# Scores for the maxima half a step later in a cross-attention kernel: heads 0 and 1 at a step's end, heads 2 and 3 in the next step, and v's third part in two pieces

## The reference

```python
x = layer_norm(hidden_states, ln1_w, ln1_b)
q = heads(x @ q_w + q_b); k = heads(ctx @ k_w + k_b); v = heads(ctx @ v_w + v_b)
attn = softmax(where(mask, q @ k.T / sqrt(32), finfo.min))
hidden = heads_back(attn @ v) @ cproj_w + cproj_b + hidden_states
y = gelu(layer_norm(hidden, ln2_w, ln2_b) @ fc_w + fc_b) @ proj_w + proj_b   # 512 -> 2048 -> 512
return hidden + y
```

## Time and profile before

| | us |
|---|---|
| median of 3 runs (757.47 to 764.28) | 763.86 |
| the profiled execution | 761.63 |
| its span in the profile | 759.8 |

### The profile page before, as it was taken

The page is one execution under the profiler, slowest core; times in us unless marked ns, Lnnn a source line. Parts: engine busy times, 40 slices in busy tenths (PEclk is TensorE's granted clock), DMA queues, the critical chain, the costliest instruction groups (busy, mean ns, idle before and its releaser), DMA issues.

```text
span 759.8 us, 13142 instructions
## 1 busy us (share of the span) xinstructions
PE 701.7 (92%) x4544; PEld 607.5 (80%) x4544; DVE 465.2 (61%) x859; ACT 321.7 (42%) x582; POOL 257.5 (34%) x219
## 2 busy tenths in 40 slices
PE   3769989899998989899789999999999999999997
PEld 3658879798888879798677888888888888888886
DVE  5487978988789898978868775533225232252222
ACT  4146766867677776857751212112121121211110
POOL 6234656655546666556743121000000001000000
PEclk9787989999999999999889999999999999999999
DMA  7685554645455454434705400010001000010001
GB/s 222 158 239 149 161 159 123 166 141 156 139 155 153 140 155 138 113 114 142 196 1 161 130 1 1 15 41 1 1 0 56 0 0 0 0 55 1 1 0 57
DMA packets 51146, 69.16 MB, mean 91 GB/s; under 512 B 8344, under 2 KB 29208, under 8 KB 51104
## 3 DMA queue, kind: packets, MB, share of 16 engines
q1 hardware_dynamic: 50832, 68.07, 31.2%
q0 software_dynamic: 272, 0.54, 0.4%
HBM read 47.21 MB, written 20.99 MB: 90 GB/s over the span
## 4 chain that ended last, share of the span: by engine, by line
PE 70%; issue 9%; DVE 8%; POOL 6%; ACT 3%; DMA 3%; SPq 2%; DVEq 0%; ACTq 0%; POOLq 0%
PE psum L1212 8%; PE psum L1213 8%; PE psum L1214 8%; PE psum L1199 8%; PE psum L1198 8%; PE psum L1197 8%; PE psum L1004 6%; PE psum L1005 5%; PE psum L1006 5%; POOL p_lo L473 4%; PE psum L1038 2%; PE psum L1095 2%; DVE negm L755 2%; PE psum L1022 1%; PE psum L1116 1%
## 5 line engine op out<-in xcount | busy, mean ns | idle before, releaser
L473 POOL TENSOR_TENSOR p_lo<-p,p_hi 128x512 f16<-128x512 f32 x128 | 156.9, 1236 | 122.5 <-ACT p_hi L559 122.2
L685 ACT ACTIVATE h<-psum,cols 128x512 f32<-128x512 f32 x64 | 44.1, 689 | 290.0 <-PE psum L1199 290.0
L942 DVE CAST h_hi<-h 128x512 fp32r<-128x512 f32 x64 | 27.9, 436 | 208.1 <-ACT h L685 208.1
L557 ACT ACTIVATE p<-psum,maskbias 128x512 f32<-128x512 f32 x128 | 88.4, 690 | 45.8 <-PE psum L1022 44.8
L1212 PE MATMUL psum<-w_mlp,h_hi 128*128 128x512 f32 x256 | 100.7, 393 | 0.9 <-DVE hidden L784 0.9
L1214 PE MATMUL psum<-w_mlp,h_lo 128*128 128x512 f32 x256 | 99.7, 390 | 0.0
L1213 PE MATMUL psum<-w_mlp,h_hi 128*128 128x512 f32 x256 | 99.7, 389 | 0.0
L1197 PE MATMUL psum<-y_hi,w_mlp 128*128 128x512 f32 x256 | 99.7, 389 | 0.0
L1199 PE MATMUL psum<-y_hi,w_mlp 128*128 128x512 f32 x256 | 99.7, 389 | 0.0
L1198 PE MATMUL psum<-y_lo,w_mlp 128*128 128x512 f32 x256 | 99.6, 389 | 0.0
L559 ACT ACTIVATE p_hi<-psum,maskbias 128x512 f16<-128x512 f32 x128 | 88.8, 694 | 0.0
(11 more groups left out here) (105 smaller groups left out, 1516.1 us busy)
## 6 DMA issues: line engine op xcount, KB each, us to landing
qk_rows<-qk SPq DMA_DIRECT2D x32, 512.0 KB, 2.7
stacks<-qk_rows SPq DMA_DIRECT2D x64, 256.0 KB
stacks<-qk_rows SPq DMA_DIRECT2D x64, 128.0 KB
hidden<-in_x_dram SPq DMA_DIRECT2D x8, 512.0 KB, 4.5
ctx_sb<-in_ctx_dram SPq DMA_DIRECT2D x8, 512.0 KB, 5.2
w_mlp_raw<-in_L_xattn_fc_w_dram SPq DMA_DIRECT2D x16, 256.0 KB, 4.6
w_mlp_raw<-in_L_xattn_proj_w_dram SPq DMA_DIRECT2D x16, 256.0 KB, 6.2
out_dram<-hidden SPq DMA_DIRECT2D x16, 256.0 KB, 2.3
```

Source lines behind the costliest of these rows:

```text
L473: pool.tensor_tensor(p_lo[:, slot, :], p32[:, u % 2, :], p_hi[:, slot, :], ALU.subtract).then_inc(s["p_lo_done"], 1)
L557: act.activation(p32[:, u % 2, :], psum[:, ST + kc, :], ACT.Exp, bias=maskbias[:, kc:kc + 1], scale=SCALE32)
```

## The change

The scores of heads 0 and 1 move to the end of the step on PE, and those of heads 2 and 3 of the same group to the next step, just behind `transposed_scores` of the first pair. `transpose_max` moves from the front part of a step to its end: in steps 0 to 2 just ahead of the second pair of `transposed_scores`, in step 3 behind the scores. DVE's `maximum` calls move with them: heads 2 and 3, with the two `m12` operations, come right behind `low_parts`, and heads 0 and 1 are last in the step. ACT's copy to `mrow` moves behind the second pair of exponentials (in step 3, behind the third). The table `USES` gets a new order. The third part of v is made in two pieces, one in step 0, one at the start of step 1. The subtraction of v's rest (L909) moves ahead of `add_hidden` in step 3. No instruction of arithmetic is added or removed, and the orders of SP and POOL stay as they are.

```diff
-        USES = [("qk", 0), ("ctx", 0), ("ctx", 1), ("m", 0), ("c", 1),
-                ("qk", 1), ("m", 1), ("att", 0), ("att", 1), ("v", 0),
-                ("qk", 2), ("m", 2), ("v", 1),
-                ("qk", 3), ("m", 3), ("c", 0), ("x", 0), ("x", 1)]
+        USES = [("qk", 0), ("ctx", 0), ("ctx", 1), ("c", 1), ("m", 0),
+                ("qk", 1), ("att", 0), ("att", 1), ("v", 0), ("m", 1),
+                ("qk", 2), ("v", 1), ("m", 2),
+                ("qk", 3), ("c", 0), ("x", 0), ("m", 3), ("x", 1)]
```

In DVE's `step`:

```diff
             def step(it, g):
+                if g == 1 and batch(it):
+                    third_part(1)
                 low_parts(it, g)
...
                 if g == 0 and batch(it + 1):
                     context_lo(it, 0)
+                maximum(it, g, (2, 3))
+                if g == 0 and batch(it + 1):
                     context_lo(it, 1)
...
                 if g != 1:
                     products_out(it, g)
-                maximum(it, g, (0, 1))
...
                     wait(dve, "v_cast", it * 2 + 1)
-                    for kc in range(KC):
-                        ins = dve.tensor_tensor(vparts[:, kc, :, 1 + 2 * HD:VW], v_heads[:, kc],
-                                                vparts[:, kc, :, 1 + HD:1 + 2 * HD], ALU.subtract)
-                    ins.then_inc(s["v_split"], 1)
+                    third_part(0)
...
                     add_values(it, g - 1)
-                last = isinstance(it, int) and (it, g) == (B - 1, 0)
-                if last:
-                    maximum(it, g, (2, 3))
+                if g == 3 and batch(it + 1):
+                    wait(dve, "v1_cast", it + 2)
+                    dve.tensor_tensor(v32[:, :, :], v32[:, :, :], v1[:, :, :], ALU.subtract).then_inc(s["v_rest"], 1)
                 if g == 0 and batch(it - 2):
                     add_hidden(it, 1)
...
                 if g == 3 and batch(it + 2):
                     affine_x(it + 2)
-                if not last:
-                    maximum(it, g, (2, 3))
-                if g == 3 and batch(it + 1):
-                    wait(dve, "v1_cast", it + 2)
-                    dve.tensor_tensor(v32[:, :, :], v32[:, :, :], v1[:, :, :], ALU.subtract).then_inc(s["v_rest"], 1)
+                maximum(it, g, (0, 1))
```

In PE's `step`:

```diff
                 if g == 0:
                     transposes(it, "ctx", 0, it + 1, ctx_sb, "ctx_loaded", 16, "ctx_tr")
+                    scores(it, g, (2, 3))
                     values(it, g)
                     transposes(it, "ctx", 1, it + 1, ctx_sb, "ctx_loaded", 16, "ctx_tr")
-                    scores(it, g, (0, 1))
+                    project_c(it, 1)
                     transpose_max(it, g)
-                    if last:
-                        transposed_scores(it, g, 1)
-                        scores(it, g, (2, 3))
-                    project_c(it, 1)
...
+                scores(it, g, (0, 1))
                 if g == 3:
+                    transpose_max(it, g)
                     transposes(it, "x", 1, it + 2, xn, "x_normed", 2, "x_tr")
-                if not (last and g == 0):
-                    scores(it, g, (2, 3))
```

More of the change, by code:

```diff
@@ L640, in step @@
                     exps(it, g, 1)
-                    maxima_out(it, g)
-                    if batch(it + 1) and not (isinstance(it, int) and it == -1):
+                    if batch(it + 1):
                         x_hi(it + 1)
@@ L651, in step @@
                     exps(it, g, 1)
-                if g == 2:
+                if g >= 2:
                     exps(it, g, 0)
                     exps(it, g, 1)
[L655 to L658, removed]
+                if g != 3:
                     maxima_out(it, g)
@@ L662, in step @@
                 exps(it, g, 2)
+                if g == 3:
+                    maxima_out(it, g)
                 exps(it, g, 3)
@@ L696, in tail @@
                 if it == B and g == 1:
-                    wait(act, "v_split", B)
+                    wait(act, "v_split", B * 2)
                     gelu(0, 0)
@@ L746, in maximum @@
             def maximum(it, g, heads):
-                G = it * NG + g + 2
+                G = it * NG + g + (2 if heads[0] == 0 else 1)
                 if not group(G):
@@ L788, in add_values @@
                 wait(dve, "v_proj", b * 2 + (t + 1))
-                wait(dve, "v_split", b)
+                wait(dve, "v_split", b * 2)
                 dve.tensor_tensor(v32[:, t, :], in_bank("v", t), vb_bc[:, :], ALU.add).then_inc(s["v_added"], 1)
@@ L850, in products_out, with third_part @@
                     dve.reciprocal(rl[:, t, h0:h0 + GH], rows[:, :, 0]).then_inc(s["pv_taken"], 1)
+            def third_part(kc):
+                dve.tensor_tensor(vparts[:, kc, :, 1 + 2 * HD:VW], v_heads[:, kc],
+                                  vparts[:, kc, :, 1 + HD:1 + 2 * HD], ALU.subtract).then_inc(s["v_split"], 1)
             def step(it, g):
+                if g == 1 and batch(it):
+                    third_part(1)
                 low_parts(it, g)
@@ L868, in step @@
                     products_out(it, g)
-                maximum(it, g, (0, 1))
-                if g == 0 and batch(it + 1) and not (isinstance(it, int) and it == -1):
+                if g == 0 and batch(it + 1):
                     x_lo(it + 1)
@@ L1034, in scores @@
                 for hh in heads:
-                    h = GH * ((g + 2) % NG) + hh
+                    h = GH * ((g + (2 if heads[0] == 0 else 1)) % NG) + hh
                     wait(pe, "max_taken", G * 4 + (hh - 1))
@@ L1105, in values @@
                 wait(pe, "p_lo_done", (G + 1) * 4)
-                wait(pe, "v_split", b + 1)
+                wait(pe, "v_split", (b + 1) * 2)
                 wait(pe, "v_cast", (b + 1) * 2)
@@ L1142, in step @@
                     transposes(it, "ctx", 0, it + 1, ctx_sb, "ctx_loaded", 16, "ctx_tr")
+                    scores(it, g, (2, 3))
                     values(it, g)
                     transposes(it, "ctx", 1, it + 1, ctx_sb, "ctx_loaded", 16, "ctx_tr")
-                    scores(it, g, (0, 1))
+                    project_c(it, 1)
                     transpose_max(it, g)
-                    if last:
-                        transposed_scores(it, g, 1)
-                        scores(it, g, (2, 3))
-                    project_c(it, 1)
                 if g == 1:
-                    transpose_max(it, g)
-                    scores(it, g, (0, 1))
+                    scores(it, g, (2, 3))
                     for j in range(2):
@@ L1160, in step @@
                 if g == 2:
+                    scores(it, g, (2, 3))
+                    values(it, g)
+                    project_v(it, 1)
                     transpose_max(it, g)
+                if g == 3:
+                    scores(it, g, (2, 3))
                     values(it, g)
[L1163 to L1172, removed]
                     if last:
@@ L1178, in step @@
                     transposes(it, "x", 0, it + 2, xn, "x_normed", 2, "x_tr")
-                if not (last and g in (0, 3)):
+                if not (last and g == 3):
                     transposed_scores(it, g, 1)
```

## The result

The changed kernel takes 801.88 us (median of 4 runs, 798.04 to 806.07) against 760.87 us for the kernel before beside it: a ratio of 1.053, 95% interval 1.048 to 1.058. Its profiled execution took 798.07 us, with a span of 796.3 us against 759.8.

What follows compares the result with a forecast made beforehand. TensorE, busy 92%, loses wherever it newly waits for in-order DVE; step terms over the iterations sum to +30.4, plus 3 for the tail, on 761.6: 795, forecast 796 us with half the median's offset, range 774 to 818.

Steps and rivals of the forecast that it cites:

- Step 0: First step of a batch: project_qk newly waits for DVE's add_hidden, 12.9 against 11.11 us, +1.8 (+0.4 to +2.9).
- Step 1: PE's 1.7 us wait goes, but the v projection waits for low_parts: 11.3 against 11.90 us, -0.6 (-1.0 to 0).
- Step 2: project_qk newly waits for DVE's add_values: 11.0 against 9.02 us, +2.0 (+1.0 to +2.6).
- Step 3: transpose_max waits for add_hidden, project_qk for ACT's mrow copy: 12.6 against 10.72 us, +1.9 (+1.2 to +3.1).
- The batch: Four steps of a full batch in the loop, 42.75 us before: +1.8 - 0.6 + 2.0 + 1.9 = +5.1 us.
- the tail: Iteration 7: transposed_scores waits for the mrow DMA, some 2.8 us beyond cover in two or three steps; +3 (0 to +6).
- rival 2: The clock joins in: one lower-clock stretch in each of six batches, +10 us, up to 825 with high ends; chance 0.14.
- rival 1: POOL and DVE fall apart in time, so the terms are their low ends: +12 us, no tail, 774; chance 0.14.
- Rival 3: Faster, 749 us: DVE reaches v_added (9.0 us into step 2) and add_hidden (about 10 into step 0) before PE asks; chance 0.06.
- rival 4: No change, 762 us: new waits as long as the old ones, those in steps 2 and 3 hidden; chance 0.06.
- the signs named: PE waits at project_qk in steps 0, 2, 3, some 6 us per batch; step 1's transpose_max wait gone; DVE about 37 us.
- The rule weighed: DVE and POOL exclude each other for whole instructions: m12 pairs could be held twice, 4 to 5 us more per batch.

Runs made afterwards that it cites:

- a_all: Changed kernel with three DVE orders edited: add_values ahead of the statistics in step 2, add_hidden earlier in steps 0 and 3; 767.6 us, ratio 1.007.
- b_split: Kernel before with only v's third part in two pieces, the second at the start of step 1; 753.72 us, ratio 0.986.
- b_split_more: b_split repeated with more rounds, against the kernel before; 754.79 us, ratio 0.989.
- a_mrow: a_all plus ACT's copy to mrow ahead of the third pair of exponentials in step 3; 764.34 us, ratio 1.002.
- a_best: a_all plus ACT's mrow copy ahead of the third exponentials in step 3 and add_hidden ahead of x_lo in step 0; 767.55 us, ratio 1.003.
- a_step0: Changed kernel with add_hidden of step 0 ahead of the first piece of v's third part on DVE; 794.45 us, ratio 1.040.
- a_step3: Changed kernel with add_hidden of step 3 ahead of products_out and v's rest on DVE; 794.16 us, ratio 1.039.
- b_vrest: Kernel before with only the subtraction of v's rest moved ahead of add_hidden in step 3; 763.58 us, ratio 1.001.

## Why the prediction was right, point by point

*The bound.* DVE's order for the most part, and not its amount of work: three DVE edits took back 31 of 36.5 us of span, some 23 of them in the lengths of the steps. Theory B, that PE's placement or the `mrow` path costs the time, fails as the main cause in a_all, but something is left of it. The change contains b_split, which helps by itself. Beside that part alone (b_split_more, 754.79 us) the best form of the whole change (a_mrow, 764.34) is 9.6 us longer at nearly the same mean clock (0.971 and 0.974). By the windows its batch takes 43.46 us against 41.83, with steps 1 to 3 longer by 0.5, 0.8 and 0.5. Whether PE's placement, the new turns of the banks or more DVE orders make these 1.6 us wasn't tested.

*The terms, against the full-clock batch.* Step 0: +1.8 forecast, +1.33 found; `m12` was disturbed little there (0.39 for the cast) and `x_lo` took 1.27 instead of 1.6. Step 1: -0.6, found -0.38. Step 2: +2.0, found +2.46: the two `m12` operations took 0.72 and 1.08, near my high end, beside POOL. Step 3: +1.9, found +1.68; `normed_x` needed only 0.99 instead of 1.94 for both tiles, as POOL's pair ended when it began (286.52 and 286.46), but the `m12` subtraction ahead of it was held until then (1.09 instead of 0.17), which I had not counted in this step. The batch: 47.85 forecast, 47.84 found; the errors of the terms cancel, so the last digits are luck.

*The sum.* The start of iteration 0 came 2.1 us later (I had 0.5), iteration 0 was 1.1 us longer (3.2 forecast), iteration 1 by 4.9, iterations 2 to 5 by 7.5, 6.4, 5.3 and 5.2, and 6 by 2.0: 34.4 in all for the forecast 30.4, the lower clock of iterations 1 to 3 included. Of the tail, from the list of waits of the changed kernel between 384 and 430 us:

```profile
PE psum L1020 <- DMA stacks<-mrow: 3.8, 3, 1.8
```

3.8 us in three waits for the `mrow` DMA, which didn't exist before. Iteration 7 to the first matmul of the MLP got longer by 3.1, as forecast (windows of the kernel before, then of the changed one):

```profile
349.81:392.49 42.68, 35.72 (x300) 30.27 (x299) 35.97 (x72) 31.57 (x62) 27.73 (x24) 0.84 0.44 124
```

```profile
384.20:429.94 45.74, 37.29 (x303) 32.52 (x304) 35.59 (x74) 30.68 (x60) 26.71 (x23) 0.78 0.42 118
```

But PE's idle time grew by only 1.5 us (8.45 against 6.96), as other waits got shorter; the other 1.6 is busy time, at a granted clock of 0.78 against 0.84. So the wait that I forecast came, it was worth half of what I gave it, and the agreement is luck.

*The rivals.* The clock (rival 2) came in by a part: six steps with a lower clock in iterations 1 to 3 and none in 4 to 6, against two and one in the kernel before, so three more at 1.5 us. With that the profiled execution took 798.07 us for the forecast 795; the other 3 us of the distance between 796 and 802 is the median, which lies 3.8 above that execution where I counted 1. The four executions took 798.07 and 798.04 us at a mean granted clock of 0.959, and 806.07 and 805.68 at 0.946 and 0.948. The disturbances (rival 1) went in part: DVE is busy 34.8 us in the batch (10.43 + 7.56 + 8.55 + 8.29) and not the 37 that I named, and they stayed where POOL works back to back, in steps 2 and 3. Rival 3 fails at both of its points, where PE waits 2.0 and 2.3 us, and rival 4 by the 5.1 us of the batch. Of the signs named, PE's waits at the first matmul of `project_qk` come to 4.3 us where I had some 6, and another 1.2 stands ahead of `transpose_max`; in step 3 PE was held at `transpose_max` and hardly by the copy to `mrow`.

*The rule weighed.* By the Trainium skill, page "SBUF — State Buffer", section "Who interferes with whom", the loser of the shared ports blocks for the winner's whole instruction. The 8-column subtraction in step 2 did (1.08 instead of 0.17 us). The x subtraction of a_best and a_all agrees as well, once POOL's two multiplications are read one by one. In a_best the first is undisturbed (1.05 us) and ends at 233.69; the x subtraction, begun 0.45 us before that, takes 1.53, against 1.22 for one of the same size alone, and POOL's second multiplication, begun while it runs, takes 2.03. In a_all the x subtraction begins first and takes 1.27, and POOL's first multiplication takes 2.01. In each pair the one that began second got longer, by 0.1 us less than the time that was left of the other.

## What to carry over

When work on an in-order engine is moved, add up everything that now stands ahead of each result that another engine needs early, from the moment when the list can start, and compare with the time at which it is asked for; that gave each step within 0.5 us here. Of an engine's list, put first what others wait for and last what nobody needs until the next round: moving three calls was worth 34 us, and the one useful part of the change, half of a subtraction moved to an idle place, 1.1 to 1.4%, a part of it through the clock. Where a wait has two conditions, putting one ahead of the other saves nothing: the later of the two counts. When a change has parts, compare the mended whole with its best part as well as with the kernel before: beside the latter a_mrow looks level, beside b_split_more it loses 9.6 us.

## What was unexpected in the hardware

The stretches of 1.2 GHz don't follow single waits. In the changed kernel the same steps with the same waits have them in iterations 1 to 3 (mean clock 0.92) and none in 4 to 6 (1.00). They cost 1.5 us each, shift when one wait is shortened, and vanish between 94 and 362 us when the steps together are 3.7 us shorter per batch. Executions of one kernel differ by them too: the changed kernel took 798 us at a mean granted clock of 0.959 and 806 at 0.947. So an edit's effect on the median can be several microseconds more or less than the difference of two spans: -7.4 with 3.4 in the span for a_step0, -7.7 with 2.3 for a_step3, where 3.8 of each difference is the changed kernel's profiled execution against its median. And an edit can change the clock of all its runs: b_vrest lengthens five steps by about 1.1 us, runs at 0.973 instead of 0.965, and loses nothing.
